# Latent attention in a two-layer decoder: the causal mask added by VectorE instead of TensorE

## What is computed

```python
q = rmsnorm(hidden_states @ q_a_w, q_a_ln_w) @ q_b_w
kv_raw = hidden_states @ kv_a_w
kv_latent = rmsnorm(kv_raw[..., :KV_LORA], kv_a_ln_w)
...
scores = jnp.einsum('bqhd,bkhd->bhqk', q, k) * scale
causal = jnp.tril(jnp.ones((T, T), bool))
scores = jnp.where(causal, scores, jnp.finfo(scores.dtype).min)
probs = jax.nn.softmax(scores, axis=-1)
attn = jnp.einsum('bhqk,bkhd->bqhd', probs, v)
return attn.reshape(B, T, NUM_HEADS * V_HEAD) @ o_w
```

## Time and profile before

| | us |
|---|---|
| median of 3 runs | 1426.25 (1425.66 to 1429.34) |
| the profiled execution, its own time | 1432.41 |
| its span | 1430.10 |
| TensorE matmul busy | 1084.7 (76%) |
| VectorE busy | 917.5 (64%) |
| ScalarE busy | 594.3 (42%) |
| GpSimd busy | 504.4 (35%) |

### The profile page before, as it was taken

The page is one execution under the profiler, slowest core; times in us unless marked ns, Lnnn a source line. Parts: engine busy times, 40 slices in busy tenths (PEclk is TensorE's granted clock), DMA queues, the critical chain, the costliest instruction groups (busy, mean ns, idle before and its releaser), DMA issues. The chain is left out here.

```text
span 1430.1 us, 28477 instructions
## 1 busy us (share of the span) xinstructions
PE 1084.7 (76%) x8985; PEld 835.4 (58%) x9056; DVE 917.5 (64%) x2412; ACT 594.3 (42%) x1306; POOL 504.4 (35%) x975
## 2 busy tenths in 40 slices
PE   5688898488763443435999999999999488876997
PEld 4466675255531221224899898989898355544665
DVE  3478895378868999991444444445444478865886
ACT  3245453188861212211332333233323078873553
POOL 5276788433322222222133223223322233322332
PEclk8889999699996667666999999999999799998999
DMA  8899986435524010002010011000100345521111
GB/s 153 175 181 210 194 167 114 124 101 139 148 64 89 30 33 27 28 26 63 12 35 27 23 29 37 22 22 29 37 18 19 91 112 134 141 80 49 55 52 41
DMA packets 138268, 112.05 MB, mean 78 GB/s; under 512 B 16848, under 2 KB 130816, under 8 KB 138176
## 3 DMA queue, kind: packets, MB, share of 16 engines
q1 hardware_dynamic: 124864, 100.01, 29.5%
q10 hardware_dynamic: 11344, 8.72, 2.3%
q0 software_dynamic: 1968, 2.16, 0.9%
HBM read 68.91 MB, written 31.52 MB: 70 GB/s over the span
## 5 line engine op out<-in xcount | busy, mean ns | idle before, releaser
L388 DVE TENSOR_REDUCE ca_nm<-ca_p_s 128x2 f32<-128x512 f32 x256 | 168.3, 684 | 43.7 <-PE ca_p_s L297 41.6
L528 ACT ACTIVATE ca_pt<-ca_p_e 128x512 f32<-128x512 f32 x256 | 139.2, 595 | 9.7 <-PE ca_p_e L317 3.9
L317 PE MATMUL ca_p_e<-ca_qs,ca_ks 128*128 128x256 bf16 x512 | 99.5, 277 | 52.3 <-ACT ca_pt L528 50.4
L297 PE MATMUL ca_p_s<-ca_ks,ca_qs 96*128 96x256 bf16 x512 | 103.0, 285 | 31.0 <-DMA ca_ks<-k_stack 31.0
L2086 ACT ACTIVATE la_pq<-la_p_s,la_nm 128x128 f32<-128x128 f32 x256 | 72.9, 368 | 106.8 <-DVE la_nm L2126 106.8
L1919 PE MATMUL la_p_f<-la_qt,q_w 128*128 128x128 f32 x512 | 101.4, 280 | 12.5 <-ACT la_lt L2067 11.3
L1577 PE MATMUL mx_p_i<-identb,mx_qi 128*128 128x128 bf16 x128 | 19.4, 307 | 106.9 <-POOL mx_qi L1428 106.9
L1920 PE MATMUL la_p_f<-la_qt,q_w 128*128 128x128 f32 x512 | 99.0, 275 | 0.0
L520 ACT ACTIVATE ca_qs<-ca_p_m 32x1024 bf16<-32x1024 bf16 x64 | 65.0, 1016 | 74.0 <-PE ca_p_m L307 73.2
L1919 PEld LDWEIGHTS la_p_f<-la_qt,q_w 128*128 128x128 f32 x512 | 77.6, 192 | 16.3 <-ACT la_lt L2067 16.3
L1428 POOL TENSOR_TENSOR mx_qi<-mx_f_rounded,mx_f_half 128x512 bf16<-128x512 bf16 x32 | 33.3, 1060 | 150.7 <-DVE mx_f_rounded L1410 150.7
(11 more groups left out here) (283 smaller groups left out, 2953.7 us busy)
## 6 DMA issues: line engine op xcount, KB each, us to landing
sa_qks<-sa_qkp SPq DMA_DIRECT2D x96, 128.0 KB, 5.1
ca_qs<-q_stack SPq DMA_DIRECT2D x32, 384.0 KB, 4.5
ca_ks<-k_stack SPq DMA_DIRECT2D x32, 384.0 KB, 5.4
ca_ct<-in_ctx_t SPq DMA_DIRECT2D x32, 128.0 KB, 5.2
ca_xr<-x_state SPq DMA_DIRECT2D x32, 128.0 KB, 2.1
x_state<-ca_xn SPq DMA_DIRECT2D x32, 128.0 KB, 2.0
k_stack<-sa_cxp SPq DMA_DIRECT2D x16, 192.0 KB, 2.8
q_stack<-sa_parts SPq DMA_DIRECT2D x16, 192.0 KB, 2.4
```

The lines of the kernel that those rows point to most:

```text
L297: last = pe.matmul(p_s[n % 3][:, qc, :], QS[b % 3][0:STACK, h, 128 * qc:128 * qc + 128], KS[b % 3][0:STACK, h, :], start=True, stop=True)
L317: last = pe.matmul(p_e[h % 2][:, kc, :], KS[(2 * i + u) % 3][:, h, 128 * kc:128 * kc + 128], QS[(2 * i + u) % 3][:, h, :], start=True, sto ...
L388: dve.tensor_reduce(NM[u][:, h, :], p_s[(H * (2 * i + u) + h) % 3][:, :, :], AX.X, ALU.max, negate=True).then_inc(max_done, 1)
L528: act.activation(PT[h // 4][:, h % 4, :, :], p_e[h % 2][:, :, :], ACT.Exp, scale=SCALE).then_inc(exp_done, 1)
```

## The change

TensorE's matmul that put the mask into the bank goes. The score products no longer accumulate on it. VectorE adds the mask to the bank's scores and writes the sum to a new pair of SBUF tiles `MS` (f32, 128 x 4 x 128), counts this in a new semaphore `masked`, waits for that count, and reduces `MS` to the maxima. The exponentials read `MS`. The bank is free for new scores once the add of the group two before has run (`masked`), and `MS` once the exponentials of the group two before have.

```diff
+        MS = [sb(f"ms{n}", [128, 4, 128], F32) for n in range(2)]
...
-                wait(pe, exp_done, n - 1)
-                pe.matmul(p_s[g % 2][:, :, :], sh.identb[:, :], sh.mask_qk[:, :, :], start=True, stop=False,
-                          skip_group_check=True)
+                wait(pe, masked, n - 1)
                 for j in range(4):
                     last = pe.matmul(p_s[g % 2][:, j, :], QQ[u][:, 4 * g + j, :], KK[u][:, 4 * g + j, :],
-                                     start=False, stop=(j == 3), skip_group_check=True)
+                                     start=True, stop=True)
...
-                    last = act.activation(PQ[g % 2][:, j, :], p_s[g % 2][:, j, :], ACT.Exp,
+                    last = act.activation(PQ[g % 2][:, j, :], MS[g % 2][:, j, :], ACT.Exp,
...
-                wait(dve, scores_ready, G * b + g + 1)
-                wait(dve, exp_done, G * (b - 2) + g + 1)
-                dve.tensor_reduce(NM[u][:, 4 * g:4 * g + 4], p_s[g % 2][:, :, :], AX.X, ALU.max,
+                n = G * b + g
+                wait(dve, scores_ready, n + 1)
+                wait(dve, exp_done, n - 1)
+                dve.tensor_tensor(MS[g % 2][:, :, :], p_s[g % 2][:, :, :], sh.mask_qk[:, :, :], ALU.add).then_inc(masked, 1)
+                dve.wait_ge(masked, n + 1)
+                dve.tensor_reduce(NM[u][:, 4 * g:4 * g + 4], MS[g % 2][:, :, :], AX.X, ALU.max,
                                   negate=True).then_inc(max_done, 1)
```

More of the change, by code:

```diff
@@ L1803, in latent_attention @@
         heads_turned, heads_act, heads_dve = sem("heads_turned"), sem("heads_act"), sem("heads_dve")
-        scores_ready, max_done = sem("scores_ready"), sem("max_done")
+        scores_ready, masked, max_done = sem("scores_ready"), sem("masked"), sem("max_done")
         exp_done, p_turned, p_copied, pv_done = sem("exp_done"), sem("p_turned"), sem("p_copied"), sem("pv_done")
```

## The result

| | before | after |
|---|---|---|
| median, us | 1427.53 (1425.66 to 1429.34, 4 runs) | 1446.78 (1441.95 to 1453.76, 4 runs) |
| ratio to before, 95% interval | | 1.0139 (1.0091 to 1.0186) |
| the profiled execution, its own time | 1432.41 | 1453.76 |
| its span | 1430.10 | 1452.0 |

The changed kernel is slower, by 19 us in these runs; 1.4% is small, but the interval lies clear of 1. A later set of 6 runs beside 11 of before on another chip gave 1447.64 against 1429.52, a ratio of 1.0121 (1.0093 to 1.0150). The forecast was 1440.0 with a range of 1429 to 1450: the direction was right and the loss, 19.3 us in the first runs and 18.1 in the later set, was a third to two fifths more than the 13.7 us of the sum.

What follows compares the result with a forecast made beforehand. TensorE nearly bounds the stage, but chains through other engines set the time where it waits. 7.5 + 4.4 + 0.7 + 0.5 + 0.6 gave +13.7 us, forecast 1440.0 us, range 1429 to 1450.

Steps and rivals of the forecast that it cites:

- TensorE's 0.22 us a group: Mask's matmul before each group's scores: removing it gives back 0.22 us a group, 14.1 us at most.
- The add and the dependent maximum at 0.72 us: VectorE, each group: add of 0.69 us plus 0.03 us of wait before the maximum that depends on it.
- 418 or 1112 ns: Bounds for VectorE's add: one-source operation in SBUF, 418 ns; two SBUF operands beside a busy GpSimd, 1112 ns.
- First place: Scores of group 0 to the projection, once a sample: 0.50 us later, 15 samples, 7.5 us.
- ScalarE's source: Exponentials reading SBUF instead of PSUM: 33 ns, taken once a group on the path, 0.6 us; upper bound four times.
- Second place: Weighing of group 1, waiting for group 0's division: 0.43 us late in 10 samples, 0.02 in 5; 4.4 us.
- The ends: Stage's start, first transposes: 0.5 us later; last sample, where the division already binds: 0.7 us.
- (c): Add dearer, 1451 us at 1112 ns; ScalarE's source exposed four times, 1.7 us more; granted clock might fall, unpriced; chance 0.15.
- (a): Rival: the chains have slack and TensorE is the bound, 1412 us; chance 0.07.
- (b): Rival: only the projection's chain binds, weighing of group 1 doesn't; +2.7 us, 1429 us; chance 0.13.
- (d): Rival: the add is as cheap as 418 ns, 7.3 us less, 1433 us; chance 0.05.

Runs made afterwards that it cites:

- `no_mask`: The kernel before without the mask's product and with nothing in its place: 1420.88 us against 1428.93, ratio 0.9953.
- `exps_psum`: The changed kernel with its exponentials reading the unmasked scores in PSUM: 1441.35 us, ratio to before 1.0081.
- `even_new`: The change for groups 0 and 2 alone, groups 1 and 3 as in the kernel before: 1444.90 us, ratio to before 1.0110.
- `product_kept`: The changed kernel with the mask's product put back on TensorE besides the add: 1450.65 us, ratio to before 1.0155.
- `odd_new`: The change for groups 1 and 3 alone, groups 0 and 2 as in the kernel before: 1430.49 us, ratio to before 1.0006.
- the first reordering: Both head copies put ahead of the next sample's group 0: 1417.32 us (0.9908) on the changed kernel, 1418.86 (0.9916) on the kernel before.
- the second reordering: Division of group 0 put ahead of group 2's maxima, run with the first reordering: 1418.91 us on the changed kernel, 1421.42 on the kernel before.

## Why the prediction was right, and where its size was not

**TensorE's 0.22 us a group:** right. `no_mask` gave 0.43 us a sample in the steps, 3.0 us in sum before the projection (group 0) and 3.0 before the weighing of group 1 (group 3), as walked through (0.44 a sample).

**The add and the dependent maximum at 0.72 us:** right. 685 ns and a start 0.72 us after the add's. Neither bound, 418 or 1112 ns, was near. The agreement with the nearest row of one PSUM and one SBUF operand held for a bf16 mask too.

**First place, 0.50 us a sample plus 0.033 for ScalarE's source:** the place was right, the size low: 9.4 us in 14 steps against 7.5. From the first weight load to the projection the two parities got longer by 0.63 us (3.99 to 4.62) and 0.73 (3.90 to 4.63). The term mis-sized is ScalarE's source: four exponentials take 0.14 us longer (1.14 to 1.28), four times the 33 ns of the earlier trace rows, which was my upper bound and not my value. I had counted the longer time of one operation once for the four; they take it four times. `exps_psum` shows it as 1.8 us in the steps. The idle time in front of the projection grew by more than forecast, from 0.56 to 1.66 us a sample instead of to 1.2: some 0.67 us of that is the longer chain, 0.22 the missing product of group 1, and the rest is open.

**Second place, 0.43 or 0.02 us:** right in place, the size high: 2.4 us in 14 steps against 4.0. In the two parities of the steady part it is 0.37 and -0.15: from the residual add to the weighing of group 1 it was 4.70 and 5.23 us, and is 5.07 in both. The five samples that I had down for 0.02 later got there a little earlier. In `even_new` and `product_kept`, which have group 3's product, they stand at about -0.02, so the gain is that product's, for which I had allowed nothing.

**The steady part in sum:** 7.0 + 0.5 for the first place and 4.0 for the second make some 11.4 us in 14 steps by the forecast, measured 11.8. That the sum is so close is luck: one place was 1.9 us dearer and the other 1.6 cheaper than forecast.

**The ends, 0.5 + 0.7 us:** the chains were right, and what the sum left out, the clock, is its largest miss. At the start the part up to the first residual add holds the first sample's projection and weighing too, some 1.0 to 1.5 us by the forecast, and at the same clock it measures 1.0; in the profile where the clock had fallen to 0.79 it is 2.6. In the last sample the weighing of group 1 starts 5.18 us after the residual add instead of 4.46, 0.72 us later, as forecast, but the sample gets 3.1 to 3.3 us longer. I had walked it at a constant clock and put the clock into rival (c) with no price. There was a row for it: the kernel before already has its last sample at a granted clock of 0.82. Its 18.8 us against the 16.4 of `no_mask` and `odd_new` at 1.00 make an estimated 2.4 us for the clock; the changed kernel's 21.9 to 22.2 against 17.2 with the first reordering, the same sample at 1.00, make 4.7 to 5.0. The difference, 2.3 to 2.6 us, is what was missing.

**Rivals.** (a) fell with `no_mask` and `product_kept`, (b) with the new wait for the division in 9 samples and with the 5.7 us that the second reordering gave, (d) with the add's 685 ns. Of (c) the add's price fell too; its two small parts, ScalarE's source four times exposed and the clock, are what the sum lacked: 16 x 0.11 = 1.8 us, and for the clock 2.3 to 2.6 us in the last sample and, in one of two profiles, 1.6 at the start.

**What stays open:** the timed runs differ by 18 to 19 us and the stage by 15.8 and 17.7 in two profiles. The rest of the program starts the stage up to 10 us earlier or later from kernel to kernel, and the changed kernel's first four runs spread over 12 us where the first three of before spread over 4. No run here was made to settle that, nor why the granted clock falls in the last sample of some kernels and not in that of others with the same waits.

## What to carry to other kernels

Before taking work off the busiest engine, ask where it waits and what chain ends there: in this kernel 95% of a stage's steady part was TensorE's, and moving 0.22 us a group from it to an add of 0.72 us elsewhere cost 1.2 to 1.4%, since two of four groups stood on such chains. Moved for the groups off the chains alone it cost nothing that could be measured, and gained nothing either. Reorder first: two copies put ahead of work that was not urgent took 24 us from the changed kernel's steps and 12 from the old one's. And price a stage's first and last pieces on their own, with the granted clock of their rows.

## What the runs showed of the hardware

A series of four exponentials of 128x128 took 1.28 us from SBUF and 1.14 from PSUM, 35 ns more for each, and one of them 390 against 368 ns. The Trainium skill ("VectorE: DVE Perf Modes", section on the TRN2 errata) gives ScalarE's fixed cost as 224 cycles from SBUF and 172 from PSUM at 1.2 GHz, an estimated 43 ns of difference. The trace agrees in kind, with 35; the measurement decides.

The granted clock stayed at 1.00 in the steady part even with 1.70 us of waiting in front of every projection, and fell to 0.50 in the last sample, after waits of 1.30 and 0.89 us. Those waits alone don't explain the fall: with the first reordering the last sample had waits of 1.31 and 0.89 us and a clock of 1.00. With the 22 added matmuls, whose results nothing reads, the clock was at 1.00 in both kernels that had them, and the last sample 4.2 to 4.6 us shorter than without them (17.7 against 21.9 and 22.2, 17.95 against 22.5).
